# A fifth group of expert weights loaded ahead, in the memory of the first attention's weights and tables

## The reference: what is computed

```python
x = x + attn_a(layernorm(x))     # 16 heads of 16, rotary on half the heads, causal
x = x + ffn(layernorm(x))        # mixture of experts
x = x + attn_b(layernorm(x))     # 16 heads of 16, full softmax
x = x + ffn(layernorm(x))        # the same mixture of experts, the same weights
# ffn: 64 experts, hidden 64, 4 experts for each token; two shared experts, hidden 256 each
g = silu(flat @ wg[e]);  u = flat @ wu[e];  routed = sum over e of comb[n, e] * ((g * u) @ wd[e])
```

## Time and profile before

| | us |
|---|---|
| median of 3 runs | 1188.19 |
| lowest and highest of them | 1181.44, 1192.4 |
| profiled execution, its time | 1184.33 |
| profiled execution, span of the profile | 1182.7 |
| PE, DVE, POOL, ACT busy | 914.3, 720.7, 489.5, 449.8 |
| expert stage of r = 0, first to last store by ACT | 408.5 to 551.8 |
| expert stage of r = 1, first to last store by ACT | 952.8 to 1093.4 |

### The profile page before, as it was taken

How to read it: one execution, slowest core, us unless ns; L and a number is a source line. 1 busy time by engine, 2 the same in 40 slices (tenths; PEclk the granted TensorE clock), 3 DMA queues, 4 the chain that set the end, 5 groups by cost and what they waited for, 6 DMA issues and landing times. The chain is left out here.

```text
span 1182.7 us, 23655 instructions
## 1 busy us (share of the span) xinstructions
PE 914.3 (77%) x7706; PEld 696.8 (59%) x7706; DVE 720.7 (61%) x1899; ACT 449.8 (38%) x957; POOL 489.5 (41%) x550
## 2 busy tenths in 40 slices
PE   3985899996999787896556699997989788899000
PEld 2764577765888576684445445545878676677000
DVE  5766877754888433344666689965698643345333
ACT  1553355562211344453233268881211144455000
POOL 3000422216477522332775342221577732231775
PEclk9997899997999898998677779999899998999555
DMA  6294799939964588973486467802623498985443
GB/s 238 43 172 80 152 187 220 233 130 256 214 184 142 174 259 255 284 234 119 118 202 186 76 94 114 116 7 70 153 99 107 158 265 257 266 260 175 118 131 115
DMA packets 159015, 197.06 MB, mean 167 GB/s; under 512 B 17328, under 2 KB 137648, under 8 KB 155824
## 3 DMA queue, kind: packets, MB, share of 16 engines
q1 hardware_dynamic: 99744, 94.56, 36.7%
q0 software_dynamic: 22848, 68.18, 18.2%
q10 hardware_dynamic: 36304, 32.84, 9.2%
HBM read 132.86 MB, written 90.18 MB: 189 GB/s over the span
## 5 line engine op out<-in xcount | busy, mean ns | idle before, releaser
L856 ACT ACTIVATE tmp<-ps 128x256 f32<-128x256 f32 (+1 forms) x328 | 145.5, 472 | 127.2 <-PE ps L809 37.3
L949 ACT ACTIVATE tmp<-ps 128x384 f32<-128x384 f32 (+1 forms) x256 | 135.6, 543 | 71.5 <-PE ps L622 46.9
L485 POOL DMA_INDIRECT xd<-big,slot x128 | 129.3, 1010 | 61.7 <-issue 37.8
L524 POOL DMA_INDIRECT big<-yd,slot x128 | 126.5, 988 | 42.7 <-issue 25.0
L453 POOL COPY arena<-negmax 24x2048 bf16<-24x2048 bf16 x32 | 60.5, 1892 | 175.8 <-ACT negmax L856 175.8
L603 PE MATMUL ps<-arena 96*128 96x256 bf16 (+1 forms) x512 | 106.2, 279 | 13.1 <-DVEq L290 10.6
L1086 DVE SCALAR_TENSOR_TENSOR X<-big,comb,X 128x256 f32<-128x256 f32 x128 | 59.2, 484 | 77.6 <-DMA big<-yd,slot 77.2
L1473 DVE SCALAR_TENSOR_TENSOR tmp<-tmp,ps 128x128 f32<-128x128 f32 x128 | 36.7, 287 | 113.2 <-ACT tmp L1017 112.5
L619 PE MATMUL ps<-arena 120*128 120x256 bf16 (+1 forms) x512 | 100.9, 265 | 0.9 <-POOL arena L453 0.3
L1483 DVE COPY tmp<-ps 128x256 f32<-128x256 f32 x128 | 53.6, 424 | 66.7 <-PE ps L838 36.4
L809 PE MATMUL ps<-ident,big 128*128 128x128 f32 x512 | 74.3, 290 | 25.0 <-ACT tmp L856 15.0
(11 more groups left out here) (173 smaller groups left out, 1906.5 us busy)
## 6 DMA issues: line engine op xcount, KB each, us to landing
big<-xd POOLq DMA_DIRECT2D x128, 256.0 KB, 4.9
arena<-parts SPq DMA_DIRECT2D x192, 128.0 KB, 6.0
xd<-zero SPq DMA_DIRECT2D x8, 2048.0 KB, 14.2
spill<-in_we SPq DMA_DIRECT2D x128, 128.0 KB
yd<-tmp POOLq DMA_DIRECT2D x64, 256.0 KB, 3.5
yd<-tmp ACTq DMA_DIRECT2D x64, 256.0 KB, 3.5
parts<-arena SPq DMA_DIRECT2D x128, 96.0 KB
arena<-in_we SPq DMA_DIRECT2D x8, 1024.0 KB, 8.9
```

Of the source, the lines that this page charges most:

```text
L485: pool.indirect_dma_start(xd[:, :], bass.IndirectOffsetOnAxis(ap=slot[:, i, k:k + 1], axis=0), xn_all[:, i, :], None).then_inc(scattered.s ...
L524: pool.indirect_dma_start(gring[n % GRING], None, yd[:, :], bass.IndirectOffsetOnAxis(ap=slot[:, b * TB + m % TB, m // TB:m // TB + 1], ax ...
L856: return act.activation(dst, src, ACT.Copy)
L949: act.activation(prob[h % 8][:, 0:n], ps[2 + h % 2][:, 0:n], ACT.Exp).then_inc(exp_ready.sem, 1)
```

## The change

The five tiles named above become parts of three larger ones, `tables` (1024 columns: `headsel`, `cs`) and `weights0`, `weights1` (2048 columns each: `wqk`, `wv`, `wo`), of the same total size. `FRING` goes from 16 to 20 pairs: the fifth place has its gate and up weights in `weights0` and its down weights in `tables`. SP therefore loads five groups ahead. In `r = 0` it now waits for the last output projection (`op_done`) before the first of them. ACT issues three groups in the expert stage, behind fixed pairs 3, 7 and 11. The six patches of `hot` are counted with the later constants, so that POOL, PE and DVE wait for both with one count (`LATER`).

```diff
-RING, XRING, YRING, FRING, GROUP = 4, 8, 4, 16, 4
+RING, XRING, YRING, FRING, GROUP = 4, 8, 4, 20, 4
+FSLOTS, FGROUPS = FRING // GROUP, FIXED // GROUP
...
-        headsel = sb("headsel", [P, 2 * KC, P])
-        cs = sb("cs", [P, 2, S])
+        tables = sb("tables", [P, 1024])
+        headsel = tables[:, 0:512].rearrange("p (c n) -> p c n", c=2 * KC)
+        cs = tables[:, 512:1024].rearrange("p (a n) -> p a n", a=2)
...
-        wqk = [sb(f"wqk{r}", [P, KC, 2 * D]) for r in range(2)]
-        wv = [sb(f"wv{r}", [P, KC, D]) for r in range(2)]
-        wo = [sb(f"wo{r}", [P, KC, D]) for r in range(2)]
+        weights = [sb(f"weights{r}", [P, 2048]) for r in range(2)]
+        wqk = [w[:, 0:1024].rearrange("p (c n) -> p c n", c=KC) for w in weights]
+        wv = [w[:, 1024:1536].rearrange("p (c n) -> p c n", c=KC) for w in weights]
+        wo = [w[:, 1536:2048].rearrange("p (c n) -> p c n", c=KC) for w in weights]
...
+        gu_slot = [arena[:, 2048 * i:2048 * i + 2048] for i in range(4)] + [weights[0][:, :]]
+        down_slot = [arena[:, 8192 + 1024 * i:9216 + 1024 * i] for i in range(4)] + [tables[:, :]]
...
+        LATER = 16 * (len(CONSTS) - len(FIRST) - 1 + 6)
...
-            i, e0 = g % (FRING // GROUP), 2 * GROUP * g
+            i, e0 = g % FSLOTS, 2 * GROUP * g
...
                 if r == 1:
                     sp.wait_ge(op1_done.sem, B)
-                for g in range(FRING // GROUP):
+                if r == 0:
+                    sp.wait_ge(op_done.sem, B)
+                for g in range(FSLOTS):
                     load_fixed(sp, g)
...
                 if r == 0:
                     pool.wait_ge(cast_done.sem, 1)
-                    pool.wait_ge(hot_in.sem, 16 * 6)
+                    pool.wait_ge(later_in.sem, LATER)
...
                     if j % 2 == 0:
-                        pe.wait_ge(*fixed_in[m // GROUP % (FRING // GROUP)](r, 80 * (m // FRING + 1)))
+                        pe.wait_ge(*fixed_in[m // GROUP % FSLOTS](r, 80 * (m // FRING + 1)))
```

More of the change, by code:

```diff
@@ L143, in build @@
         cload = arena[:, 0:5 * P]
-        fixed_gu = [arena[:, 512 * i:512 * i + 512].rearrange("p (t n) -> p t n", t=2) for i in range(FRING)]
-        fixed_d = [arena[:, 8192 + 256 * i:8448 + 256 * i] for i in range(FRING)]
+        gu_slot = [arena[:, 2048 * i:2048 * i + 2048] for i in range(4)] + [weights[0][:, :]]
+        down_slot = [arena[:, 8192 + 1024 * i:9216 + 1024 * i] for i in range(4)] + [tables[:, :]]
+        fixed_gu = [gu_slot[i // GROUP][:, 512 * (i % GROUP):512 * (i % GROUP) + 512].rearrange("p (t n) -> p t n", t=2) for i in range(FRING)]
+        fixed_d = [down_slot[i // GROUP][:, 256 * (i % GROUP):256 * (i % GROUP) + 256] for i in range(FRING)]
         spill = sb("spill", [P, 3072])
@@ L231, in build @@
         neg_out, neg_spread = signal("neg_out", 16), signal("neg_spread", 16)
-        hot_in, hot_ready = signal("hot_in"), signal("hot_ready", 3)
+        hot_ready = signal("hot_ready", 3)
         s2_done, exp_ready, pv_done = signal("s2_done", 128), signal("exp_ready", 128), signal("pv_done", 32)
@@ L248, in build @@
         sd_done, sx_added = signal("sd_done", 8), signal("sx_added", 8)
-        fixed_in = [signal(f"fixed_in{i}", 80 * FIXED // FRING) for i in range(FRING // GROUP)]
+        fixed_in = [signal(f"fixed_in{i}", 80 * len(range(i, FGROUPS, FSLOTS))) for i in range(FSLOTS)]
         over_in = [signal(f"over_in{i}", 64 * FIXED // RING) for i in range(RING)]
@@ L263, in build @@
         FIRST = ("ident", "rotm", "headsum", "headsel", "cs", "gain", "wqk0", "wv0")
[L264 to L265 removed]
+        CONSTS = [(cload, "cload"), (ident[:, :], "ident"), (rotm[:, :], "rotm"), (headsum[:, :], "headsum"), (headsel, "headsel"),
+                  (cs, "cs"), (gain[:, :], "gain"), (bproj[:, :], "bproj"), (rw[:, :, :], "rw"),
                   (rb[:, :], "rb"), (iot[:, :], "iot"), (jcol[:, :], "jcol"), (swg[:, :, :], "swg"),
@@ L268, in build @@
         for r in range(2):
-            CONSTS += [(wqk[r][:, :, :], f"wqk{r}"), (wv[r][:, :, :], f"wv{r}"), (wo[r][:, :, :], f"wo{r}")]
+            CONSTS += [(wqk[r], f"wqk{r}"), (wv[r], f"wv{r}"), (wo[r], f"wo{r}")]
+        LATER = 16 * (len(CONSTS) - len(FIRST) - 1 + 6)
         x_tiles = t["x"].rearrange("b (t p) d -> p (b t) d", p=P)
@@ L306, in load_fixed @@
         def load_fixed(e, g):
-            i, e0 = g % (FRING // GROUP), 2 * GROUP * g
-            gu = arena[:, 2048 * i:2048 * i + 2048].rearrange("p (e n) -> p e n", e=2 * GROUP)
-            dn = arena[:, 8192 + 1024 * i:9216 + 1024 * i].rearrange("p (m a n) -> p m a n", m=GROUP, a=2)
+            i, e0 = g % FSLOTS, 2 * GROUP * g
+            gu = gu_slot[i].rearrange("p (e n) -> p e n", e=2 * GROUP)
+            dn = down_slot[i].rearrange("p (m a n) -> p m a n", m=GROUP, a=2)
             e.dma_start(gu, t["we"][e0:e0 + 2 * GROUP, :, 0:4 * FF].rearrange("e p n -> p e n")).then_inc(fixed_in[i].sem, 16)
@@ L337, in _ @@
                 for half in range(2):
-                    sp.dma_start(hot[KR + 8 * part:KR + 8 * part + 8, 8 * half:8 * half + 8], t["ident"][0:8, 0:8]).then_inc(hot_in.sem, 16)
+                    sp.dma_start(hot[KR + 8 * part:KR + 8 * part + 8, 8 * half:8 * half + 8], t["ident"][0:8, 0:8]).then_inc(later_in.sem, 16)
             sp.wait_ge(setup_done.sem, 2)
@@ L591, in _ @@
                     pe.wait_ge(cast_done.sem, 1)
-                    pe.wait_ge(later_in.sem, 16 * (len(CONSTS) - len(FIRST) - 1))
+                    pe.wait_ge(later_in.sem, LATER)
                 def scores(b, h):
@@ L1192, in _ @@
                 if r == 0:
-                    dve.wait_ge(later_in.sem, 16 * (len(CONSTS) - len(FIRST) - 1))
+                    dve.wait_ge(later_in.sem, LATER)
                 def group(b, g):
```

## The result

The change makes the kernel a little faster: 1174.13 us median of 10 runs (1167.13 to 1182.61) against 1187.44 us of 10 (1178.29 to 1192.4), a ratio of 0.9909 with a 95% interval from 0.9881 to 0.9937. That is 10.8 us (7.5 to 14.1) by the ratio and 13.3 by the two medians. Forecast were a median of 1178.1 and a gain of 10.1 us.

A forecast was written before the change was run, and what follows sets the result against it. TensorE was taken as the floor of the expert stages, 3.987 us a pass, with stalls behind ACT's loads. 10.7 - 0.6 = 10.1 us off 1184.33 gives 1174.2 profiled; 3.9 more gives a median of 1178.1, range 1169 to 1186.

The forecast's parts named there:

- The fourth load's price, step one: Expert stages of both runs: removing ACT's load behind pair 15 gives back 7.0 + 3.7 = 10.7 us, bounds 3.6 and 15.5.
- The sign that the three loads left cost between 2 and 8 us each: Expert stages: ACT's remaining loads were to cost between 2 and 8 us each, as before the change.
- Two halves of the loss: Expert stages: issuing makes ACT's copies 5.30 us late; later ACT waits 3.67 us for a `yd` store queued with weights.
- The ahead side of r = 0: SP's queue before the expert stage: first load 6.3 us later, zeroing of `yd` 11.8 us later, all hidden.
- The 0.6 us for the scatters: POOL's scatters in r = 0: about nine more in the busy DMA stretch, 0.06 us each; bounds nothing and 11.8 us.
- the rival of the backlog: SP's longer queue, 17.5 us in both runs, delays POOL's scatters: 6.8 us slower, 1195.0; chance 0.06.
- One sign of being wrong: POOL in r = 0: the prediction is wrong if reading `xd` starts later than 394.
- The new wait of POOL: POOL's first `mark_heads` waits for all later constants: a few us at most, covered by its 92.13 us idle; zero cost.
- The rival of the page's byte price: Expert stage loads: bytes at 436 GB/s make 3.6 us each, 7.2 us back for two, profiled time some 1177.7; no separate chance.
- The level: Whole kernel: profiled time 1174.2; the median of the runs lies 3.9 us above the profiled execution, so 1178.1.
- little comes back: Expert stages: each removed load returns only 1.8 to 3.7 us, 3.6 to 7.4 in all, median 1183.3; chance 0.24.
- more comes back: Expert stages: the removed loads return 15.5 us, as the two dearest cost, median 1173.3; chance 0.20.

## Why the prediction was right

**The fourth load's price, step one.** Forecast 10.7 us from its two stalls in one execution, with bounds 3.6 and 15.5. Shown: with the fourth load out and four passes at the floor in its place, the ratio gives 10.8; with it put back, 1.0004. The reading that a stall belongs to the load ahead of it was sound. That the number agreed so well is partly luck: single loads cost from 1.7 to 10.7 us, and a stage with four loads lasted 143.3, 142.8 and 139.6 us for r = 0 in three kernels and 140.6, 140.0 and 134.6 for r = 1. The stages of the profiled execution gained 9.4 us and not 10.7. The mean of 5.0 us would have forecast 10.0, and the 4.4 of the kernel without loads 8.8. The sign that the three loads left cost between 2 and 8 us each failed for one, with 10.7.

**Two halves of the loss.** ACT's block and the stores behind the weights were both named. The runs size them, by the stages: with SP as the issuer 13.1 of 29.7 us go and 16.6 stay, and tiny transfers leave 5.7. What I did not see is that they are dearer together, 29.7 against 16.6 + 5.7 = 22.3. Nor did I see that a long stall can leave TensorE at the lower clock level for the matmuls behind it (3.59 instead of 1.92 us for 32 of them).

**The ahead side of r = 0.** Forecast: SP's loads 6.3 us later, the zeroing 11.8, hidden, and 0.6 us at the scatters. The loads began 8.3 us later, mostly since this time the last projection ran at the lower clock level (granted clock 0.55, where before it was 1.00):

```profile
271.82 3.58 PE L669 MATMUL ps<-weights,tmp 128*128 128x256 f32 x8 [0.69 <-ACT tmp L864]
```

instead of 1.99 us, and the fifth group took 7.4 us instead of 5.5: the zeroing came 15.3 us later. It was hidden all the same. The slower projection is not the change's doing. The kernel before with pieces, which has the old tiles, shows it too:

```profile
275.95 3.59 PE L663 MATMUL ps<-wo,tmp 128*128 128x256 f32 x8 [0.69 <-ACT tmp L858]
```

while the change in r = 0 alone and the kernel with the load put back, which have the new tiles, took 1.99. The 0.6 us for the scatters was not there. With it goes the rival of the backlog: it needed more than 10.7 us to reach POOL, and no part of it did.

One sign of being wrong did come up: `xd` was read first at 395.86, later than the 394 that the prediction had set. The 2.9 us are not the backlog. The scatters had started 3 us late and taken as long as before, and with five groups ahead and the projection at the upper level `xd` was read at 392.77. The kernel before with pieces, with four groups ahead, read it at 399.99. The sign was set too close to the scatter between executions.

**The new wait of POOL** shows as forecast, 2.09 us, and is covered:

```profile
22.84 7.14 POOL L434 CAST arena<-hot 24x4096 bf16<-24x4096 f32 x2 [2.09 <-DMA weights<-in_wo]
```

**The rival of the page's byte price.** The Trainium skill, "DMA: Bandwidth & Descriptors", section "Anatomy of one DMA — SWDGE (gpsimd) path", gave an estimate of 3.6 us a load. That section is on transfers issued by GpSimd, and these are issued by ACT. The 42 loads cost 5.0 on the mean. And the runs show that the rule asks the wrong question here: the same bytes cost 1 to 2 us a load in three pieces. The same page, section "Issuing engines are not separate DMA queues", says that transfers of SP, ACT and POOL run on the same DMA engines and interleave, so that another issuer saves only the time of issuing, usually small beside the transfer. The trace agrees that they share: with SP as the issuer a store still held up ACT's copies for 4.53 us. The saving was not small here, 13.1 of 29.7 us in the stages.

**The level.** The profiled execution was forecast at 1174.2 and took 1175.8; the median was forecast at 1178.1 and is 1174.1. The 3.9 us that I added, because the median of three runs lay above the profiled one, were scatter: ten runs have a median of 1187.4, and the change's own median lies below its profiled execution. By the ratio, "little comes back" and "more comes back" both lie outside the interval, the first just below its lower edge (7.4 against 7.5), the second above its upper (15.5 against 14.1). By the median alone it would be less clear: 1174.1 is nearer to the 1173.3 of "more" than to the 1178.1 of the forecast.

## What to carry to other kernels

A prefetch inside a stage that runs at an engine's floor is paid for by what it holds up, not by its size: look at the iteration time behind each load, and at the store or copy that shares its issuer and its DMA engines. Before finding memory to move one load out of the stage, cut the loads into pieces that fit into one iteration. Here three pieces gave 24 us without the extra buffer, where the buffer alone gave 11; the buffer with three pieces gave 25 and with four 34 to 36. With three pieces in place the buffer gave nothing that could be measured. When one execution has the same event eight times, take the mean for the forecast and the extremes for the range.

## What the runs showed of the hardware that was not expected

- A 256 KB store issued right behind 1.5 MB of loads in the same queue took 12.75 us on the chain, with a median of 3.5 us for all such stores; with the loads in another queue, a store issued during their burst took 10.0 us to land, and a copy waited 4.53 us for it.
- The indirect scatters kept their pace while more was moved beside them: 44 in 56 us with the DMA engines 0.44 busy before and 0.63 after.
- Behind 4.36 us in which TensorE sat idle, 32 matmuls of 128 x 128 took 3.59 us at a granted clock of 0.53 instead of 1.92.
- The last output projection of r = 0, the same work on TensorE, took 1.99 us at a granted clock of 1.00 in one execution and 3.58 at 0.55 in another. What decides between them stays open.
- On one chip the kernel before took 1296 us instead of 1187, while a pass of the expert stage stayed at 3.98 us. In the change's trace there, the time is lost between 310 us and the first store (457.06 instead of 410.80) and between the expert stages (460.7 instead of 399.5); behind the last store it is 89.4 us on both chips. Three activations by ACT (L996) in that first stretch waited 56 us in all for something that the profile cannot name ("another core or an unknown queue"). The cause stays open.
